# An AdaLN, Mamba and tree-FFN kernel on one core: another order of the prologue's loads, products and gate values, and a later step for the second norm's statistics

## The reference

```
ga = (2*(ga >= 0) - 1) * max(|ga|, 0.25)          # gb likewise
h  = layernorm(x) * (1 + ca) + sa
x  = x + ga * mamba(h)
h  = layernorm(x) * (1 + cb) + sb
x  = x + gb * tree_ffn(h)

mamba(h):     xp, z = split(h @ W_in)                       # 256 and 256 channels
              u = silu(causal_conv(xp, conv_w, 4 taps) + conv_b)
              dt_r, B, C = split(u @ W_xp)                   # 8, 16, 16
              delta = softplus(dt_r @ W_dt + dt_bias)
              state[n] = exp(delta*A[n]) * state[n] + delta*u*B[n]    # over tokens, n = 0..15
              y = sum_n C[n]*state[n] + u*D_skip
              return (y * silu(z)) @ W_out
tree_ffn(h):  gate = sigmoid((h @ Wq.T) @ routers.T)         # 255 nodes, depth 8
              leaf_prob = product of gate or 1-gate along each path    # 256 leaves
              return (leaf_prob @ leaf_values) @ Wout_w.T + Wout_b
```

## Time and profile before

| | us |
|---|---|
| median of 3 runs | 499.08 (497.8 to 499.5) |
| the profiled execution | 498.78 |
| its span in the trace | 496.5 |
| VectorE busy in the span | 451.4 (91%) |
| GpSimd busy | 428.1 (86%) |
| TensorE busy | 412.8 (83%) |
| ScalarE busy | 375.7 (76%) |

### The profile page before, as it was taken

The page is one execution under the profiler, slowest core; times in us unless marked ns, Lnnn a source line. Parts: engine busy times, 40 slices in busy tenths (PEclk is TensorE's granted clock), DMA queues, the critical chain, the costliest instruction groups (busy, mean ns, idle before and its releaser), DMA issues. The chain is left out here.

```text
span 496.5 us, 6734 instructions
## 1 busy us (share of the span) xinstructions
PE 412.8 (83%) x2163; PEld 281.4 (57%) x2163; DVE 451.4 (91%) x537; ACT 375.7 (76%) x685; POOL 428.1 (86%) x240
## 2 busy tenths in 40 slices
PE   8979666995699698996899788997899698667887
PEld 5437444663458455663658455674658455554654
DVE  5998899979999899989999889988999889999961
ACT  2478975688768798688968898788967797388754
POOL 4869899999999789979999799978999789989700
PEclk9999978998889889998999999997999998797999
DMA  7583045200930027300741017300741027200001
GB/s 178 142 288 163 1 145 219 86 0 7 325 118 2 1 69 297 108 0 2 271 145 55 2 69 297 106 1 0 267 158 47 1 61 305 106 2 0 21 1 42
DMA packets 23714, 51.06 MB, mean 103 GB/s; under 512 B 4473, under 2 KB 13824, under 8 KB 19584
## 3 DMA queue, kind: packets, MB, share of 16 engines
q1 hardware_dynamic: 23680, 50.64, 29.4%
HBM read 48.01 MB, written 2.62 MB: 102 GB/s over the span
## 5 line engine op out<-in xcount | busy, mean ns | idle before, releaser
L584 POOL TENSOR_TENSOR hc<-h,c_rows 128x1024 f32<-128x1024 f32 x126 | 296.4, 2370 | 25.3 <-DVE h L1333 25.3
L1333 DVE TENSOR_TENSOR_SCAN h<-dA,state,dbu 128x512 f32<-128x512 f32 x192 | 233.3, 1262 | 3.7 <-ACT dA L672 3.7
L672 ACT ACTIVATE dA<-delta,a_neg 128x512 f32<-128x512 f32 x256 | 173.9, 686 | 52.0 <-DVE h L1333 51.5
L1105 PEld LDWEIGHTS yb<-ident,hc 128*128 128x128 f32 x1024 | 132.8, 150 | 64.9 <-issue 44.0
L1105 PE MATMUL yb<-ident,hc 128*128 128x128 f32 x1024 | 157.9, 290 | 7.9 <-POOL hc L584 6.7
L1346 DVE TENSOR_TENSOR dbu<-du,bb 128x1024 f32<-128x1024 f32 x88 | 105.3, 1196 | 2.8 <-PE bb L1130 2.4
L571 POOL TENSOR_TENSOR dbu<-du,b_rows 128x1024 f32<-128x1024 f32 x40 | 94.8, 2371 | 3.9 <-DMA b_rows<-bc_dram 3.9
L1333 DVE TENSOR_TENSOR_SCAN h<-dA,dbu 128x512 f32<-128x512 f32 x64 | 74.1, 1203 | 4.0 <-ACT dA L672 3.9
L1130 PE MATMUL bb<-b_parts,sel 128*128 128x512 bf16 x88 | 35.1, 399 | 48.7 <-DVE dbu L1346 47.8
L1005 PE MATMUL mf<-f_hT,w_conv 128*128 128x512 f32 x112 | 53.4, 601 | 2.0 <-ACT zu L732 1.4
L1130 PEld LDWEIGHTS bb<-b_parts,sel 128*128 128x128 bf16 x88 | 8.8, 100 | 61.3 <-DVE dbu L1346 41.6
(11 more groups left out here) (202 smaller groups left out, 543.9 us busy)
## 6 DMA issues: line engine op xcount, KB each, us to landing
c_rows<-bc_dram SPq DMA_DIRECT2D x32, 1024.0 KB, 8.1
b_rows<-bc_dram SPq DMA_DIRECT2D x40, 256.0 KB, 9.4
xs<-in_L_attn_x_dram SPq DMA_DIRECT2D x8, 256.0 KB, 4.1
out_dram<-xs SPq DMA_DIRECT2D x7, 256.0 KB, 5.8
ygT<-in_L_attn_conv_w_dram SPq DMA_DIRECT2D x1, 512.0 KB, 5.4
bc_dram<-xd SPq DMA_DIRECT2D x8, 64.0 KB, 1.6
probT<-in_L_wmod_dram SPq DMA_DIRECT2D x1, 384.0 KB, 4.3
w_in<-in_L_attn_W_in_dram SPq DMA_DIRECT2D x1, 256.0 KB, 4.5
```

The lines of the kernel that those rows point to most:

```text
L584: nc.gpsimd.tensor_tensor(hc[:, pair % RC, :, :], h[:, pair % RH, :, :], c_rows[:, q, n % NQ, :].unsqueeze(1).broadcast_to([P, HALVES, T]) ...
L672: nc.scalar.activation(dA[ke % RD][:, :], delta[:, ge % 2, half, :], ACT.Exp, scale=a_neg[:, half, n:n + 1]).then_inc(s_dA, 1)
L1105: last = nc.tensor.matmul(bank[:, tile], hc[:, pair % RC, half, tile], ident[:, :], start=False, stop=n == N - 1, is_transpose=True, skip_ ...
L1333: v.tensor_tensor_scan(h[:, pair % RH, half, :], dA[k % RD][:, :], dbu[:, pair % RW, half, :], start, ALU.mult, ALU.add).then_inc(s_scan, 1)
```

## The change

- `T_STATS` goes from 12 to 14, `WARM_START` from 9 to 6.
- The taps come as one row of 4 KB (`tap_row`) and TensorE broadcasts them: two products of a row of ones with 512 columns each, into `dA[0]` and `dA[2]`, from which VectorE reads them.
- The columns sa and ca are loaded and multiplied first; sb and cb follow with the rest of `w_mod` and the z half of `w_in` (`s_wlate`), into `mt`.
- The conv weights are made half by half, eight multiplies of 128 columns; GpSimd's wait for `TAPS` of them is as before.
- The gate products are split by sequence: one half where all were, one half behind `u_product(1)`.
- `dskip` is loaded with the bias columns, x of groups 2 and 3 right after `w_xp`, with a semaphore of their own; x of groups 4 to 7 is waited for in group 0, step 19.
- On VectorE the statistics of groups 2 and 3 and the gates' copy stand ahead of B's first cast, and the gate values in two pieces between B's casts.

```diff
-    T_GATE, T_STATS, T_RSTD, T_OFF, T_XHAT = (4, 5), 12, 19, 20, 24
+    T_GATE, T_STATS, T_RSTD, T_OFF, T_XHAT = (4, 5), 14, 19, 20, 24
-    WARM_START = 9
+    WARM_START = 6
+        tap_row = sb("tap_row", [1, DI * TAPS])
...
-            load(w_mod[:, :, :], wmod.rearrange("k (j d) -> k j d", j=6), s_wmod)
-            load(w_in[:, :], W_in, s_wcv)
-            load(taps[:, :, :].rearrange("p e k -> p (e k)"),
-                 conv_w.rearrange("e o k -> (e o k)").partition_broadcast(P), s_wcv)
+            load(tap_row[:, :], conv_w.rearrange("e o k -> o (e k)"), s_taps)
+            mod_v = wmod.rearrange("k (j d) -> k j d", j=6)
+            load(w_mod[:, 0:2, :], mod_v[:, 0:2, :], s_wmod)
+            load(w_in[:, 0:DI], W_in[:, 0:DI], s_wu)
+            load(w_mod[:, 2:6, :], mod_v[:, 2:6, :], s_wlate)
+            load(w_in[:, DI:2 * DI], W_in[:, DI:2 * DI], s_wlate)
...
             load(dtb[:, :], dt_bias.rearrange("(h p) -> p h", p=P), s_wcol)
+            load(dskip[:, :], D_skip.rearrange("(h p) -> p h", p=P), s_wcol)
             load_x(1)
...
+            load_x(2)
+            load_x(3)
...
 TensorE
+            def broadcast_taps():
+                pe.wait_ge(s_taps, 16)
+                for half in range(HALVES):
+                    last = nc.tensor.matmul(dA[2 * half][:, :], ones[0:1, :], tap_row[:, half * T:(half + 1) * T],
+                                            start=True, stop=True)
+                last.then_inc(s_tapb, 1)
+            def modulation_products(bank, first):
+                for m in (first, first + 1):
+                    last = nc.tensor.matmul(bank[:, (m - first) * BATCH:(m - first + 1) * BATCH], w_mod[:, m, :],
+                                            c_silu[:, :], start=True, stop=True)
+                last.then_inc(s_modp, 1)
...
             def dt_weight_products():
                 pe.wait_ge(s_wdtc, 1)
+                pe.wait_ge(s_wconv, TAPS)
...
             def u_product(half):
                 for tap in range(TAPS):
-                    if half == 0:
-                        pe.wait_ge(s_wconv, tap + 1)
+                    pe.wait_ge(s_wconv, half * TAPS + tap + 1)
...
             def first_group():
-                modulation_products()
+                broadcast_taps()
+                pe.wait_ge(s_csilu, 1)
+                pe.wait_ge(s_wmod, 16)
+                modulation_products(yb[0], 0)
+                pe.wait_ge(s_wlate, 16 * n_late)
+                modulation_products(mb["t"][0], 3)
                 pe.wait_ge(s_fxh, 1)
                 turn_x(mb["f"][0], s_tr0)
                 dt_weight_transposes()
-                gate_products()
+                gate_products(0)
                 pe.wait_ge(s_h0, 1)
                 u_product(0)
                 dt_weight_products()
                 u_product(1)
+                gate_products(1)
...
                 pe.wait_ge(s_fxh, 2)
+                pe.wait_ge(s_modc, 2)
                 turn_x(mb["t"][0], s_tr1)
...
 VectorE
+            def mod_columns(bank, first):
+                dve.wait_ge(s_modp, 1 + first // 3)
+                chain(v.tensor_copy(mod_col[:, first:first + 2, :],
+                                    bank[:, 0:2 * BATCH].rearrange("p (m b) -> p m b", b=BATCH)))
+                v.tensor_scalar(mod_col[:, first + 1, :], mod_col[:, first + 1, :], 1.0, None,
+                                ALU.add).then_inc(s_modc, 1)
...
                 front_normalise(0)
-                dve.wait_ge(s_modp, 1)
...
-                for tap in range(TAPS):
-                    v.tensor_tensor(w_conv[:, tap, :], w_in[:, 0:DI], taps[:, :, tap], ALU.mult).then_inc(s_wconv, 1)
+                mod_columns(yb[0], 0)
+                dve.wait_ge(s_wu, 16)
+                dve.wait_ge(s_tapb, 1)
+                for half in range(HALVES):
+                    mine = slice(half * P, (half + 1) * P)
+                    taps = dA[2 * half][:, :].rearrange("p (e k) -> p e k", k=TAPS)
+                    for tap in range(TAPS):
+                        v.tensor_tensor(w_conv[:, tap, mine], w_in[:, mine], taps[:, :, tap],
+                                        ALU.mult).then_inc(s_wconv, 1)
+                mod_columns(mb["t"][0], 3)
...
-                gates()
                 dve.wait_ge(s_wdtp, 1)
                 v.tensor_copy(w_xdt[:, :, :],
...
-                gate_values()
-                dve.wait_ge(s_w, 16 * n_rest)
+                dve.wait_ge(s_wcol, 16 * n_col)
                 for hh in range(HALVES):
                     last = v.tensor_scalar(diag_d[:, hh, :], ident[:, :], dskip[:, hh:hh + 1], None, ALU.mult)
                 last.then_inc(s_diag, 1)
+                dve.wait_ge(s_x2, 32)
+                stats(2, f_bn, f_mv[:, 2, :, :], s_fvar)
+                stats(3, f_bn, f_mv[:, 3, :, :], s_fvar)
+                gates()
                 dve.wait_ge(s_xd0, 1)
                 v.tensor_copy(b_parts[:, 0, :], mb["f"][0][:, :]).then_inc(s_hi, 1)
-                dve.wait_ge(s_x, 16 * (GROUPS - 2))
-                stats(2, f_bn, f_mv[:, 2, :, :], s_fvar)
+                gate_signs()
...
-                stats(3, f_bn, f_mv[:, 3, :, :], s_fvar)
+                gate_values()
...
                     if 4 <= g + 4 < GROUPS and s == N_STATS:
+                        if g == 0:
+                            dve.wait_ge(s_x, 16 * (GROUPS - 4))
```

More of the change, by code:

```diff
@@ L194, in bass_adaln_mamba_tree_ffn_kernel @@
         probT = sb("probT", [P, 2, T])
-        taps = ygT[:, :, :].rearrange("p a (b k) -> p (a b) k", k=TAPS)
         rout = yg[:, 0, 0:2 * DM].rearrange("p (i d) -> p i d", i=2)
@@ L263, in bass_adaln_mamba_tree_ffn_kernel @@
         s_wmod = sem("modulation_weights_loaded")
-        s_wcv = sem("conv_weights_loaded")
+        s_wu = sem("u_weights_loaded")
+        s_taps = sem("taps_loaded")
+        s_tapb = sem("taps_broadcast")
+        s_wlate = sem("other_modulation_and_z_weights_loaded")
+        s_x2 = sem("x_of_groups_2_and_3_loaded")
         s_c = sem("c_loaded")
@@ L364, in by_dve @@
             return pair - by_pool(pair)
[L366 removed]
+        n_late, n_dt, n_col, n_xp, n_rest = 2, 2, 4, 4, 14
         @block.sync
         def _(sp):
[L370 removed]
+            count = {s_c: 0, s_taps: 0, s_wmod: 0, s_wu: 0, s_wlate: 0, s_wdtl: 0, s_wcol: 0, s_wxp: 0, s_w: 0}
             def load(dst, src, which=s_w):
@@ L396, in _ @@
                 load(w_xp[:, :, row:row + width], xp_v[:, :, first:first + width], s_wxp)
-            load(dskip[:, :], D_skip.rearrange("(h p) -> p h", p=P))
+            load_x(2)
+            load_x(3)
             load(w_out[:, :, :], W_out.rearrange("(h p) d -> p h d", p=P))
@@ L407, in _ @@
                 load(rout[rows:2 * rows, :, :], routers[first:first + 2 * rows, :].rearrange("(h r) d -> r h d", h=2))
-            assert list(count.values()) == [1, 1, n_conv, n_dt, n_col, n_xp, n_rest]
-            for g in range(2, GROUPS):
+            assert list(count.values()) == [1, 1, 1, 1, n_late, n_dt, n_col, n_xp, n_rest]
+            for g in range(4, GROUPS):
                 load_x(g)
@@ L864, in _, with gate_products @@
             pe.wait_ge(s_const, 1)
-            def modulation_products():
-                pe.wait_ge(s_wmod, 16)
-                pe.wait_ge(s_csilu, 1)
-                for m in range(6):
-                    last = nc.tensor.matmul(yb[0][:, m * BATCH:(m + 1) * BATCH], w_mod[:, m, :], c_silu[:, :],
-                                            start=True, stop=True)
+            def broadcast_taps():
+                pe.wait_ge(s_taps, 16)
+                for half in range(HALVES):
+                    last = nc.tensor.matmul(dA[2 * half][:, :], ones[0:1, :], tap_row[:, half * T:(half + 1) * T],
+                                            start=True, stop=True)
+                last.then_inc(s_tapb, 1)
[3 more added lines that the diff above has]
+                                            c_silu[:, :], start=True, stop=True)
                 last.then_inc(s_modp, 1)
-            def gate_products():
+            def gate_products(b):
                 pe.wait_ge(s_cwide, 1)
-                for b in range(BATCH):
-                    for i, m in enumerate((2, 5)):
-                        last = nc.tensor.matmul(yb[1][:, (2 * b + i) * DM:(2 * b + i + 1) * DM], c_wide[:, b, :],
-                                                w_mod[:, m, :], start=True, stop=True)
+                for i, m in enumerate((2, 5)):
+                    last = nc.tensor.matmul(yb[1][:, (2 * b + i) * DM:(2 * b + i + 1) * DM], c_wide[:, b, :],
+                                            w_mod[:, m, :], start=True, stop=True)
                 last.then_inc(s_gatep, 1)
@@ L1271, in first_group @@
                 front_normalise(0)
-                dve.wait_ge(s_modp, 1)
-                chain(v.tensor_copy(mod_col[:, :, :], yb[0][:, 0:6 * BATCH].rearrange("p (m b) -> p m b", b=BATCH)))
```

(7 more changed lines are left out.)

11 lines of the change are left out of this document (5 added, 6 removed).

## The result

| | before | after |
|---|---|---|
| median (lowest to highest of 20 runs each) | 499.29 us (497.8 to 500.74) | 497.26 us (495.12 to 498.75) |
| ratio to before, 95% interval | | 0.9967 (0.9956 to 0.9978) |
| the profiled execution | 498.78 | 497.06 |
| its span | 496.5 | 494.8 |
| first scan | 30.03 | 30.00 |

The kernel is 1.65 us faster (499.29 x 0.0033; 1.1 to 2.2), where 4.6 were forecast (499.08 less 494.5). The lower part of the table says where the rest went: behind step 13 of group 0 the new kernel is 3.4 us shorter, where 3.1 were forecast; before it 1.7 are lost, where 1.3 should have been won. One disturbed execution of 2201.76 us, in experiment 5, where the others of its kernel took 495 to 498 us, is left out of all ratios.

The account below looks back on a forecast made before the run. VectorE was taken to wait for others in the prologue and to set the pace in eight groups. 498.78 - 3.1 (statistics) - 1.3 (prologue) = 494.4, forecast as 494.5 us; range 492.4 to 497.3.

Parts of the forecast that it names:

- The move of the statistics: VectorE's groups: scan 13 still waits for its exponential, scan 15 starts earlier; 0.52 us gained in each of six groups, -3.1 us.
- Rival B: Scan 13's stall in the groups keeps its whole length, only renamed to an exponential: 497.5 us; chance 0.12.
- rival D: VectorE's whole wait for the copy into `xs` goes, 12.2 us: 485.3 us; chance 0.05.
- The prologue: Before the groups: B's first cast 1.6 us earlier, less 0.3 for gate operations, -1.3 us; bounds -2.4 and +2.4.
- rival C: Prologue gains nothing or loses (0 to +2.4 us), by a lower-level broadcast or held gate operations: about 496.5 us; chance 0.12.
- the start of group 0: Later loads, stores, fills and scans hang on B's last casts, so they move with these one for one.
- I take the middle, 10.2: TensorE's prologue: start of `u_product(0)`, between 11.8 at the lower and 8.6 at the upper clock level; gain 1.5 us.
- The level of `u_product(0)`: TensorE's prologue: this product takes 3.70 us like its twin instead of 4.56, another 0.86 us gained.
- VectorE's chain: VectorE's prologue work ahead of B's first cast: ready for it at 20.6 us, at worst 22.2.
- the late columns: VectorE's prologue: the later-arriving modulation columns add 0.35 us.
- Gates in B's gaps, +0.3: VectorE between B's casts: four gate operations cost 2.2 us, fitting with the casts into 4.24; +0.3 us, 1.9 if held.
- The base: Starting time of the sum: the profiled execution of the kernel before, 498.78 us, 0.3 under the median of 499.08.

Follow-up runs that it names:

- experiment 5: Changed kernel with the taps' 512 KB load back, behind the late weights, and no broadcast: ratio to before 0.9946, again 0.9943.
- the repeat: The changed kernel once more, unaltered, for a second profile and more timed runs: ratio to before 0.9957.
- experiment 1: Kernel before with only `T_STATS` moved from 12 to 14, run twice: ratio to before 0.9944 and 0.9941.
- experiment 10: Kernel before with ScalarE's block of table loads and SiLUs in step 11, dt products a step later, `T_STATS` 13: ratio 0.9836, 490.95 us against 498.82.
- experiment 9: Changed kernel with all gate products behind the prologue, gate values in group 0, statistics of groups 2 and 3 back between B's casts: ratio to before 0.9982.
- experiment 8: Kernel of experiment 5 with eight dummy products of 128 rows ahead of the modulation products: ratio to before 0.9965.
- experiment 3: Changed kernel with 14 dummy products in three of TensorE's gaps between 28 and 37 us: ratio to before 0.9979.
- experiment 4: Changed kernel with the third and fourth gate operation moved into group 0, ahead of the `dbu` multiply of state 4: ratio to before 0.9974.
- 7: Changed kernel with `WARM_START` back at 9: ratio to before 0.9961.
- 6: Kernel of experiment 5 with the second `mod_columns` (sb and cb) ahead of the conv weights on VectorE: ratio to before 0.9942.
- 11: Kernel before with the changes of experiment 5's prologue and experiment 10's block together: ratio to before 0.9874.

## Why the prediction was right and wrong

**The move of the statistics: right, mechanism and size.** 0.52 x 6 = 3.1 us less were forecast; alone it measured 2.8 and 2.9. Behind scan 13 of group 0 the profile shows 3.4 us less than before, the repeat 3.4 too, and the two of experiment 1 show 2.0 and 3.5. Rival B (a stall of full length) and rival D (all 12.2 us go) are out: the wait shrank from 2.05 to 1.54 us a group, and all waits of both rows from 19.8 to 16.7. That ScalarE's block is what is late, experiment 10 showed: once it stands a step later, scan 13 runs inside it and 8.2 us go.

**The prologue: wrong in sign.** Forecast -1.3; alone it measured +0.8 and +1.3. This is rival C, its prologue part between 0 and +2.4, with a chance of 0.12. The range given, 492.4 to 497.3, still holds the measured median of 497.26. That is luck: the forecast was wrong on the prologue, and the range reached so far up to take in rival C.

In the profiles the change is worth 1.7 us and not the 4.4 of the sum (3.1 + 1.3): 0.3 more from the statistics, 1.3 less up to the first scan (30.00, forecast 28.7), and 1.7 less between the first scan and scan 13 of group 0, for which the sum has no term. So two steps failed: the level of TensorE in the prologue, and the start of group 0, taken to move with the first scan one for one. By steps:

- *"I take the middle, 10.2"* is the step that failed. The two levels gave 11.8 and 8.6 for `u_product(0)`; 11.59 came. No profile of the new kernel lies between: the four untouched ones all have 11.59. And the upper value, reached in experiment 9 (8.46), was paid back by a clock of 0.50 in the product itself. The reason given, work without a gap from 1.31 on, did not hold: seven of eight broadcasts took 3.78, the lower level.
- *The level of `u_product(0)`* was to give 0.86; it gave 0.61 (3.95 for 4.56) in this profile and nothing in the second one (4.61).
- *VectorE's chain* was put at 20.6 and at worst 22.2 for B's first cast; it came to 22.05. Its terms were off both ways: the tap multiplies cost 1.67 and not 2.6 but began at 9.02 and not 8.0, the late columns 1.80 and not 0.35, held by GpSimd's memset, which started earlier since it waits for four of now eight multiplies. `a_neg` ended at 17.49, not 16.3. The diagonals cost 0.96, not 0.5. VectorE was ready 0.3 ahead of the x_dbl product's end, so with VectorE as it was a quicker TensorE would have won 0.4 us at most, and the cast would have missed its 21.4 all the same. In experiments 5 and 8, with TensorE quicker and the taps by load, VectorE was the bound.
- *Gates in B's gaps, +0.3*: the four operations took 3.32 and not 2.2 us. Between the casts lie 4.80 instead of 4.24: +0.56.
- *The base.* The profile of before was the slowest of five old prologues, by 0.6 us against their mean. A gain read against it is too large by that.
- *Not seen at all*: the fall of the granted clock near 33 us, a term that the sum puts at nothing. Where no fillers, gate work or moved block disturb group 0, scan 13 follows the first scan after 24.1 us without a fall (24.5 in experiment 8, at a clock of 0.95) and after 25.8 to 26.6 with it. In the profile of the new kernel this is the whole of the 1.7 us lost ahead of scan 13; the first scan is where it was (30.00, before 30.03).

## What stays open

The clock fell near 33 us in all four profiles of the new prologue as it stands and in two of five of the old one, in one of four with the taps by load and in experiment 9, and in none of 3, 4 and 7. Whether the new prologue makes the fall likelier, or whether four of four is chance, these runs don't settle, nor how much of the +0.8 to +1.3 it is. The distance of the first scans (0.9 us) would cover most of it by its size. But the prologue with the taps by load has its first scans as late (29.86 to 30.43 in experiments 5, 6, 8 and 11) and costs nothing in 5 and 6, and what it has less of is the fall; this speaks for the fall, on one profile a run. A profile is one execution: the twelve timed ones of the repeat lie in two clusters, six from 494.9 to 496.0 us and six from 498.4 to 498.5, and the profiled one is of the upper cluster. What parts the clusters is not shown. Nor is it shown why the level rose early in three of five old prologues, in one of eight with a broadcast and in one of three with the taps by load and no dummies.

## What to carry to other kernels

When the wait of an engine is renamed by a reorder, the gain is the work that moved into the stall, and it can be read from the order of time before anything is built; the larger gain lies with the block that is late, here a few constants away. In a prologue, work out both clock levels, forecast one of them, and take the base from several profiles: here the same instructions put the first scan anywhere between 28.70 and 30.03. Moving work into VectorE's gaps was free only where GpSimd was idle too: the last gate operation took 0.69 us in the prologue and 2.74 beside GpSimd in group 0. And the sum of a prologue should not end at the first scan: here 1.7 us were lost behind it.

## What the runs showed of the hardware

- Tiny operations are held like large ones: `TENSOR_SCALAR` on 128x2 took 0.17 us at 8.94 and 1.64 us at 10.81, beside a `MEMSET` of GpSimd of 1.80. A `SCALAR_TENSOR_TENSOR` of 128x512 took 0.69 at 26.50 and 2.74 beside GpSimd's multiply (experiment 4). The Trainium skill (SBUF — State Buffer, "SBUF: two separate sides") has the two engines share a port pair, held for a whole instruction; these rows agree, and the first shows it for a GpSimd operation that only writes.
- TensorE's records can be at the lower level while the profile shows a granted clock of 1.00: six bf16 products of 512 columns took 2.74 us at the start (0.43 each) and 1.47 at 34.82 in experiment 3; four f32 records of the broadcast took 3.78 in seven profiles and 2.03 in one.
- The same list of instructions up to 4 us gave a broadcast of 3.78 us six times and of 2.03 once (experiment 9). In five of the six profiles where the level was up early the granted clock was down soon after: 0.50 from 8 to 14 us in that one, 0.72 to 0.74 in four; experiment 8's had 0.95.
